# Attention: row maxima taken in two halves, and the next unit's scores issued between the present unit's shifts

## The reference

```
scores = einsum('bhqd,bhkd->bhqk', qh, kh) * scale
attn   = softmax(scores, axis=-1)          # exp(s - max(s)) / sum
out    = einsum('bhqk,bhkd->bhqd', attn, vh)
```

## Time and profile before

| what | value |
|---|---|
| median of 3 runs | 1122.9 us (1122.15, 1127.29, 1122.9) |
| profiled execution | 1127.73 us |
| its span, first to last instruction | 1126.0 us |
| mean granted clock of PE in it | 0.985 |
| PE busy | 1036.6 us (92%) |
| DVE busy | 534.3 us (47%) |
| ACT busy | 461.4 us (41%) |
| POOL busy | 268.2 us (24%) |

### The profile page before, as it was taken

The page is one execution under the profiler, slowest core; times in us unless marked ns, Lnnn a source line. Parts: engine busy times, 40 slices in busy tenths (PEclk is TensorE's granted clock), DMA queues, the critical chain, the costliest instruction groups (busy, mean ns, idle before and its releaser), DMA issues.

```text
span 1126.0 us, 20813 instructions
## 1 busy us (share of the span) xinstructions
PE 1036.6 (92%) x8679; PEld 733.8 (65%) x8679; DVE 534.3 (47%) x1245; ACT 461.4 (41%) x715; POOL 268.2 (24%) x409
## 2 busy tenths in 40 slices
PE   7998965998999999999999999888999999999997
PEld 4655643554456666666765665666677668999996
DVE  5577687886347778753324313766321223300000
ACT  6767544665345555544123225555212222122220
POOL 3023201010113334324023100455511102222211
PEclk9999986999999999999999999999999999999999
DMA  8600000000051000000000011000710317755510
GB/s 254 84 2 2 1 1 1 1 1 1 1 134 17 2 2 3 2 2 1 1 0 1 1 49 45 3 2 2 224 38 1 113 38 271 258 172 196 172 56 1
DMA packets 55359, 60.56 MB, mean 54 GB/s; under 512 B 23603, under 2 KB 47071, under 8 KB 55266
## 3 DMA queue, kind: packets, MB, share of 16 engines
q1 hardware_dynamic: 52322, 52.93, 15.5%
q0 software_dynamic: 2944, 6.30, 1.8%
HBM read 54.76 MB, written 7.21 MB: 55 GB/s over the span
## 4 chain that ended last, share of the span: by engine, by line
PE 74%; DVE 17%; ACT 5%; issue 2%; DMA 1%; SPq 1%; POOL 0%; DVEq 0%; POOLq 0%
PE ps L1676 15%; DVE small L782 12%; PE ps L1895 10%; PE ps L2037 7%; PE ps L2050 7%; PE ps L1814 5%; PE ps L1554 4%; PE ps L1535 4%; PE ps L1713 3%; PE ps L1816 2%; PE ps L1970 2%; PE ps L1545 2%; PE ps L1532 2%; PE ps L1470 2%; ACT r_a L1219 2%
## 5 line engine op out<-in xcount | busy, mean ns | idle before, releaser
L782 DVE TENSOR_REDUCE small<-ps 128x16 f32<-128x1920 f32 (+1 forms) x64 | 142.3, 2224 | 70.4 <-PE ps L1535 50.1
L1676 PE MATMUL ps<-r_w,r_k 128*128 128x256 f32 x512 | 113.2, 381 | 2.5 <-ACT r_k L1371 2.5
L1895 PE MATMUL ps<-r_a,r_w 128*128 128x512 f32 x256 | 112.1, 594 | 3.1 <-ACT r_a L1289 3.1
L1676 PEld LDWEIGHTS ps<-r_w,r_k 128*128 128x128 f32 x512 | 96.4, 190 | 18.6 <-issue 4.4
L1583 PE MATMUL ps<-r_a,onesf 128*32 128x256 f32 (+1 forms) x768 | 81.3, 385 | 8.2 <-ACT r_a L1208 8.2
L2037 PE MATMUL ps<-r_a,w_block 128*128 128x128 f32 x736 | 86.4, 275 | 1.1 <-ACT r_a L1432 0.7
L1895 PEld LDWEIGHTS ps<-r_a,r_w 128*128 128x128 f32 x256 | 48.2, 190 | 60.2 <-issue 56.0
L2037 PEld LDWEIGHTS ps<-r_a,w_block 128*128 128x128 f32 x736 | 85.6, 192 | 2.6 <-ACT r_a L1432 1.0
L1371 ACT ACTIVATE r_k<-ps,pvec 128x512 f32<-128x512 f32 x64 | 44.0, 687 | 100.6 <-PE ps L1895 100.6
L2050 PE MATMUL ps<-w_all,r_a 128*128 x368 | 83.2, 379 | 0.2 <-issue 0.2
L1440 ACT ACTIVATE r_a<-ps 128x512 f32<-128x512 f32 x46 | 27.5, 597 | 129.3 <-PE ps L2037 117.9
(11 more groups left out here) (265 smaller groups left out, 1773.4 us busy)
## 6 DMA issues: line engine op xcount, KB each, us to landing
w_block<-in_L_ffn_W SPq DMA_DIRECT2D x23, 1024.0 KB
w_all<-in_L_ffn_W SPq DMA_DIRECT2D x8, 1024.0 KB, 9.2
r_w<-in_L_xattn_a_li_w SPq DMA_DIRECT2D x4, 1024.0 KB, 7.3
x_rows<-x_all SPq DMA_DIRECT2D x4, 512.0 KB, 3.0
x_rows<-r_a SPq DMA_DIRECT2D x4, 512.0 KB, 3.0
x_all<-in_x SPq DMA_DIRECT2D x3, 512.0 KB, 6.1
y_all<-in_L_ffn_w_gate SPq DMA_DIRECT2D x1, 1024.0 KB, 8.8
y_all<-in_L_ffn_w_up SPq DMA_DIRECT2D x1, 1024.0 KB, 11.2
```

What stands on the lines that cost most here:

```text
L782: step(dve.tensor_reduce(nm.rearrange("p (j s) -> p j s", j=4), src, AX.X, ALU.max, negate=True))
L1676: ins_ = pe.matmul(o[:, t // 2, (t % 2) * D:(t % 2 + 1) * D], src[:, c, t * P:(t + 1) * P], w[:, c, :], start=(c == 0), stop=(c == chunks ...
L1895: ins_ = pe.matmul(o, LI[a]["li2"][:, c, m * P:(m + 1) * P], FT3[:, c, :], start=(c == 0), stop=(c == KC - 1))
```

## The change

Three things are different. The DVE reduction of a unit is cut in two: first banks 2 and 3, as soon as s_done shows two strips, then banks 0 and 1. The scores of a unit are issued in the order strips 2 and 3, then strips 0 and 1. And within the loop the scores of unit n+1 no longer stand behind all shifts of unit n but between them: shifts of strips 0 and 1 for x = 0, scores of strips 2 and 3 for the first half of the queries, shifts of strips 0 and 1 for x = 1, scores of strips 2 and 3 for the second half; then the wait for os_ready; then scores of strips 0 and 1, shifts of strips 2 and 3, and so on. The wait for os_ready therefore stands behind the first two strips' scores, and in front of the shifts of strips 2 and 3. No matmul is added or removed; one DVE instruction with one wait is added per unit.

```diff
-                    dve.wait_ge(sem["s_done"], 4 * n + 4)
-                    src = bank(n % 2, 0, 4)
...
-                    step(dve.tensor_reduce(nm.rearrange("p (j s) -> p j s", j=4), src, AX.X, ALU.max, negate=True))
+                    for done, j in ((2, 2), (4, 0)):
+
+                        dve.wait_ge(sem["s_done"], 4 * n + done)
+                        src = bank(n % 2, j, 2)
...
+                        ins_ = dve.tensor_reduce(nm.rearrange("p (j s) -> p j s", j=4)[:, j:j + 2, :], src, AX.X, ALU.max, negate=True)
+                    step(ins_)
...
                 def scores(n):
-                    a, b, m = UNIT_OF[n]
-                    if n >= 2:
-                        pe.wait_ge(sem["os_ready"], n - 1)
-                    for t in range(T):
-                        for j in range(4):
...
+                    for strips in ((2, 3), (0, 1)):
+                        for t in range(T):
+                            scores_of(n, strips, t)
...
-                def shifts(n):
-
-                    a = UNIT_OF[n][0]
+                def shifts_of(n, h, x):
+
                     nk = nkeys(n)
...
+                def shifts_and_scores(n, banks_free):
+
                     pe.wait_ge(sem["maxT_ready"], n + 1)
...
+                    shifts_of(n, 0, 0)
+                    if banks_free is None:
+                        shifts_of(n, 0, 1)
+                        shifts_of(n, 1, 0)
+                        shifts_of(n, 1, 1)
+                        return
+                    if n == TOTAL_AT:
+                        shifts_of(n, 0, 1)
+                        pe.wait_ge(sem["wtot_used"], 1)
+                        scores_of(n + 1, (2, 3), 0)
+                    else:
+                        banks_free()
+                        scores_of(n + 1, (2, 3), 0)
+                        shifts_of(n, 0, 1)
+                    scores_of(n + 1, (2, 3), 1)
+                    if n >= 1:
+
+                        pe.wait_ge(sem["os_ready"], n)
+                    scores_of(n + 1, (0, 1), 0)
+                    shifts_of(n, 1, 0)
+                    scores_of(n + 1, (0, 1), 1)
+                    shifts_of(n, 1, 1)
...
-                        if n0 < n < n1:
-                            scores(n)
+                        if n > n0:
+                            shifts_and_scores(n - 1, None if n == n1 else banks_free if n == n0 + 1 else lambda: None)
...
-                            shifts(n)
```

More of the change, by code:

```diff
@@ L777, in maxima @@
                     nm = sa(NMX, 8 * pp)
-                    dve.wait_ge(sem["s_done"], 4 * n + 4)
-                    src = bank(n % 2, 0, 4)
-                    src = src.rearrange("p j (s k) -> p j s k", s=2) if pp == 1 else \
-                        src[:, :, 0:4 * KV].rearrange("p j (s k) -> p j s k", s=4)
-                    step(dve.tensor_reduce(nm.rearrange("p (j s) -> p j s", j=4), src, AX.X, ALU.max, negate=True))
+                    for done, j in ((2, 2), (4, 0)):
+                        dve.wait_ge(sem["s_done"], 4 * n + done)
+                        src = bank(n % 2, j, 2)
+                        src = src.rearrange("p j (s k) -> p j s k", s=2) if pp == 1 else \
+                            src[:, :, 0:4 * KV].rearrange("p j (s k) -> p j s k", s=4)
+                        ins_ = dve.tensor_reduce(nm.rearrange("p (j s) -> p j s", j=4)[:, j:j + 2, :], src, AX.X, ALU.max, negate=True)
+                    step(ins_)
                     nm = nm.rearrange("p (j t s) -> p t j s", t=T, j=4)
@@ L1519, in first_queries, with scores_of @@
                         ins_.then_inc(sem["q0_done"], 1)
-                def scores(n):
-                    a, b, m = UNIT_OF[n]
-                    if n >= 2:
-                        pe.wait_ge(sem["os_ready"], n - 1)
-                    for t in range(T):
-                        for j in range(4):
[L1528 to L1538, removed]
+                def scores_of(n, strips, t):
+                    a = UNIT_OF[n][0]
+                    for j in strips:
+                        o = bank(n % 2, j)
+                        if a == "a2":
+                            for x in range(2):
+                                at = 2 * KV * t + KV * x
+                                ins_ = pe.matmul(o[:, at:at + KV], queries(n, j, x, t), keys(n, j, x), start=True, stop=True,
+                                                 tile_position=(32 * j, 0))
+                        else:
+                            ins_ = pe.matmul(o[:, column(n, t)], queries(n, j, 0, t), keys(n, j), start=True, stop=True,
+                                             tile_position=(32 * j, 0))
+                        if t == 1:
+                            ins_.then_inc(sem["s_done"], 1)
+                def scores(n):
+                    for strips in ((2, 3), (0, 1)):
+                        for t in range(T):
+                            scores_of(n, strips, t)
                 def max_transposes(n):
@@ L1555, in key_scores @@
                                       tile_position=(32 * j, 0))
-                def shifts(n):
-                    a = UNIT_OF[n][0]
+                def shifts_of(n, h, x):
                     nk = nkeys(n)
+                    for j in (2 * h, 2 * h + 1):
+                        ins_ = pe.matmul(bank(n % 2, j)[0:nk, column(None, x)],
+                                         sel[32 * j:32 * j + 32, 0 if UNIT_OF[n][0] == "a1" else x, 0:nk],
+                                         maxT[32 * j:32 * j + 32, :], start=False, stop=(x == 1), tile_position=(32 * j, 0))
+                        if x == 1:
+                            ins_.then_inc(sem[f"z_done{h}"], 1)
+                def shifts_and_scores(n, banks_free):
                     pe.wait_ge(sem["maxT_ready"], n + 1)
```

## The result

The changed kernel takes 1122.5 us (median of 20 runs, 1118.4 to 1124.6), the kernel before, on the same chip, 1125.0 us (20 runs, 1122.2 to 1128.8). The ratio is 0.9977, with an interval of 0.9966 to 0.9988: some 2.6 us are gained where 12.6 were forecast, and 1122.5 lies above the range (1104 to 1118). The interval leaves out 1, but by the bound of 0.5% it is no change.

The account below looks back on a forecast made before the run. The attentions were taken as bound by a loop through DVE, not by PE's work. Gains of 6.5 (a1), 5.3 (a2) and 0.8 (L0) summed to 12.6 us, for a median of 1110 us, range 1104 to 1118.

Parts of the forecast that it names:

- What bounds the kernel: Attentions: a loop through DVE sets the pace; in a1 5.59 us, against about 5.35 through exponential and values.
- The split: DVE reduction cut into two halves: costs 0.03 us a unit, bounds 0 and 0.14, since the halves overlap.
- rival A: DVE: the two half reductions don't overlap, costing 0.14 us a unit; 7 us gained, 1116 us; chance 0.12.
- Scores of strips 2 and 3 without shifts ahead: Attention loop on PE: these scores end 0.24 us sooner, so the first reduction starts that much earlier.
- a1: Attention with 31 steps: gains 0.21 us a unit, 6.5 us, if the first exponential is not delayed.
- Do the strips run free of each other?: PE: a strip's waiting records let later ones of other strips pass; 32 records in 1.28 us as evidence.
- rival C: Everywhere, PE's path takes over: values wait for later exponentials by 0.24 us; within 5 us, 1119 us; chance 0.09.
- a2: Attention whose scores waited for out_copy: eight of 16 start earlier, gaining 0.36 us a unit, 5.3 us in all.
- rival B: In a2 and L0 the late second exponential becomes the bound; 8 us gained, 1115 us; chance 0.12.
- L0: Attention with weight work on ACT and DVE: ACT limits the gain to 0.8 us, bounds -1 and 2.5.
- The sign of being wrong: Attentions: the forecast is wrong if, among other signs, exponentials come later by more than 0.3 us.
- D: PE: matmuls start in written order across strips, delaying second exponentials; 16 us slower, 1139 us; chance 0.05.

Follow-up runs that it names:

- The three placements: Second shift of strips 0 and 1 ahead of strips 2 and 3's scores (1114.6 us), behind their first half (changed kernel, 1122.5), behind both halves (1149.5).
- both shifts first: Against the changed kernel, both shifts of strips 0 and 1 stand ahead of the next unit's first scores: 1114.6 us, ratio 0.9915 to before.
- the last experiment: Both shifts of strips 0 and 1 first, plus shifts of strips 2 and 3 ahead of the os_ready wait: 1115.5 us, ratio 0.9909 to before.

## Why the prediction was wrong

*What bounds the kernel.* Right: two loops of nearly one length, and 0.24 us of room in the one through exponential and values (0.31 with the 0.07 of the transposes). With the exponential 0.24 us later the room was gone but for that 0.07. The "some 135 us" is a rounded 12% of the span; 11.5% of it is 130.

*The split.* Taken at 0.03 us, bounds 0 and 0.14. The pair lasts 2.35 us where one took 2.29: 0.06. Right in kind (the halves overlap by 0.07), dearer by 0.03; rival A, halves that don't overlap at 0.14, is out.

*Scores of strips 2 and 3 without shifts ahead.* Right for the reduction: 0.25 us earlier. The rise of s_done that it waits for comes 0.31 us sooner in a1 (2.43 against 2.74 us after the transposes): 0.23 by the scores, and 0.08 by waiting for two rises in place of four, a term that the prediction did not have. The end of normalise takes the rest back.

*Do the strips run free of each other?* This is the step that failed, and with it the condition it carried, "if the first exponential is not delayed". The row used as evidence, 32 records in 1.28 us, shows when matmuls start and how they overlap. I took from it that written order costs nothing between strips. What ACT waits for is a completion, and no row that I had read told of a waited-for matmul against what another strip had written ahead of it. The three placements give 1.80, 2.03 and 2.52 us in a1, with the shift starting at one place throughout. The Trainium skill has the missing half of the rule: "MATMULs start and complete in program order" ("PSUM — Partial Sum Buffer", "Engine vs sequencer instructions"). The trace agrees with it on completion (z_done0 at 356.10, behind s_done at 356.06, with the shift's end at 355.38) and not on the start (that shift at 355.09, score records written ahead of it up to 355.64). I had weighed the rule on order as one piece and dropped all of it on a row that spoke of the start alone.

*a1.* Forecast 6.5 us, measured 2.2. It is rival C as written: "values wait for later exponentials by the 0.24 us that a1 has idle". With both shifts first, a1 gives 174.66 - 168.91 = 5.75 us.

*a2.* Forecast 5.3, measured 1.0, or 2.5 without the stretch at the lower clock. The reduction came 0.39 us earlier as forecast, but both exponentials late; the second by 0.54, beyond the 0.2 to 0.5 allowed, and the 0.66 us of idle time did not cover that and the gain. That is rival B's place: the late second exponential, of which 0.48 us is late telling by the last experiment. With all shifts early a2 gives 90.02 - 85.12 = 4.9.

*L0.* Forecast +0.8, measured -1.65: its exponential is 0.25 us later, and ACT's loop had no room for that, as the step itself had said. With both shifts first it gives 82.30 - 81.62 = 0.7.

*Sum.* 12.6 forecast, by stages 3.0 measured (-1.65 + 2.2 + 2.5). The version with all shifts early gives 0.7 + 5.75 + 4.9 = 11.35 by stages, and its medians 1124.7 - 1115.5 = 9.2. That is another order than the one forecast, so it does not bear the forecast out; it shows that the gain was there, a tenth under the forecast by stages and a quarter under by the medians, and that the order chosen lost it. Of the signs named, the first exponential at the same distance failed everywhere. The sign of being wrong, exponentials more than 0.3 us late, came up in a2 (0.34 and 0.54); in a1 and L0 the 0.23 to 0.25 stayed under it, too wide a threshold for a loop with 0.24 of room.

*Rivals.* C had 0.09, though it differed from the forecast by one untested assumption. The chance of "within 0.5%" (0.10) was too low by the same. D, starts in written order, did not come: the shifts start ahead of score records written before them, and a1's second exponential lost 0.24 us, not more than 0.3. It had the right rule for the wrong end of the matmul.

What stays open: the ends of matmuls are modelled, so no run shows whether the shift's data, too, arrive late, or only their semaphore. That the semaphore is late and follows those of the matmuls written ahead is shown by its events, by the starts of ACT and by one strip holding up as long as two; that all four orders keep PE's starts in place is shown as well. The mechanism inside is not.

## What to carry to other kernels

Where matmuls of separate strips overlap, ask for each semaphore what is written ahead of the matmul that raises it, even on other strips: put the matmul that another engine waits for ahead of work that merely fills PE. A row that shows free starts says nothing of completions; look at the start of the waiting engine against the start of the matmul it waits for. Semaphores that several strips raise at once come one after the other, so spread them out where an engine waits for the last. And where two loops differ by 0.24 us, write down what the change does to both before counting a gain in one.

## What the runs showed of the hardware

- A waited-for matmul on strips 0 and 1 with 0, 2 or 4 records of each other strip written ahead of it raised its semaphore so late that ACT started 0.35, 0.58 and 1.06 us after that matmul's start in a1, while that start stayed 1.45 us behind the transposes.
- In the order with four records ahead, the semaphores rose as written and not as started: s_done of strips 2 and 3 at 356.02 and 356.06, z_done0 at 356.10 and 356.13, though the shifts that raise z_done0 started at 355.09, ahead of the last of those scores (355.64).
- Rises of one semaphore by four strips that end within 0.02 us of each other come 0.04 us apart (2.61, 2.65, 2.70, 2.74 us after the transposes in a1 before). With two of them over early the last came at 2.65, and the reduction started at 2.74 instead of 2.82.
- Sixteen records on each of two pairs of strips, pair behind pair, took 1.81 us in a2 of the kernel with the split only; the second pair started 0.56 us behind the first. In the order of before the same 32 records took 1.28 us.
- Two independent reductions of 1024 columns from PSUM take 2.35 us back to back; each alone shows as 1.21 to 1.22.
